# Cross attention on one core: the first pass in pairs of matmuls on two 64-row halves of a 128-row stack, each pair set right behind a group of value sums

## The reference, cut to what matters

```python
q = split_heads(x @ qw + qb)            # 2 batches, 16 heads, 256 queries, width 16
k = split_heads(ctx @ kw + kb)          # 4096 keys
v = split_heads(ctx @ vw + vb)
scores = einsum('bqhd,bkhd->bhqk', q, k) / 4 + mask      # layer 0
scores = einsum(...) * 16**-0.5 + (i - j) * w_rel[h]     # layer 1: a bias by distance
out = einsum('bhqk,bkhd->bqhd', softmax(scores), v)
```

## Time and profile before

| what | value |
|---|---|
| device time, median of 3 | 1697.72 us (1696.73 to 1702.26) |
| profiled execution, from first to last instruction | 1696.4 us |
| granted TensorE clock, mean | 0.979 |
| PE busy | 1610.3 us (95%) |
| DVE busy | 1139.9 us (67%) |
| ACT busy | 861.8 us (51%) |
| the two cross attentions (first exponential to last copy of sums) | 258 to 656 us and 1114 to 1513 us |

### The profile page before, as it was taken

One profiled execution on the slowest core, in us unless ns is written; L12 is line 12 of the kernel. 1 busy time (PEld: TensorE's weight loads), 2 busy tenths in 40 slices (PEclk: granted clock), 3 DMA queues, 4 the chain that ended last, 5 costly groups with the idle time before them and its releaser, 6 DMA issues. The chain is left out here.

```text
span 1696.4 us, 36130 instructions
## 1 busy us (share of the span) xinstructions
PE 1610.3 (95%) x12499; PEld 972.6 (57%) x12509; DVE 1139.9 (67%) x2013; ACT 861.8 (51%) x1784; POOL 287.9 (17%) x372
## 2 busy tenths in 40 slices
PE   9999999999999997998989999889999999989697
PEld 4444444544545444674868999644454454545496
DVE  6777788888888884738553111388888888845621
ACT  3222216777777775742531111257777777765332
POOL 1422220000000001020202444220000000000053
PEclk9999999999999999999989999989999999999898
DMA  6578756434334324300038999753443434204075
GB/s 204 179 204 219 207 164 135 67 56 71 59 62 68 56 38 135 60 1 1 1 132 267 335 309 311 231 94 58 70 61 59 71 56 66 46 1 102 13 219 143
DMA packets 150745, 196.29 MB, mean 116 GB/s; under 512 B 30426, under 2 KB 123964, under 8 KB 144624
## 3 DMA queue, kind: packets, MB, share of 16 engines
q1 hardware_dynamic: 141864, 188.83, 45.3%
q0 software_dynamic: 6720, 4.31, 1.5%
q10 hardware_dynamic: 2064, 1.87, 0.3%
HBM read 156.49 MB, written 41.39 MB: 117 GB/s over the span
## 5 line engine op out<-in xcount | busy, mean ns | idle before, releaser
L1225 ACT ACTIVATE probs<-ps 128x512 f32<-128x512 f32 x1024 | 558.4, 599 | 179.0 <-PE ps L1128 166.6
L1251 DVE TENSOR_REDUCE top<-ps 128x1 f32<-128x1024 f32 x504 | 594.1, 1220 | 61.4 <-PE ps L1107 47.6
L1128 PE MATMUL ps<-qst,kst 105*128 105x256 bf16 x2048 | 353.9, 276 | 7.6 <-DVE qst L1256 2.5
L1107 PE MATMUL ps<-kst,qst 105*128 105x512 bf16 x1008 | 305.0, 385 | 6.6 <-DVE top L1251 4.0
L1128 PEld LDWEIGHTS ps<-qst,kst 105*128 105x128 bf16 x2048 | 170.3, 100 | 228.0 <-ACT probs L1225 87.1
L1142 PE MATMUL ps_o<-probs,vst 128*32 128x256 f32 x4096 | 274.1, 385 | 2.3 <-ACT probs L1225 2.3
L1142 PEld LDWEIGHTS ps_o<-probs,vst 128*32 128x32 f32 x4096 | 106.8, 109 | 113.2 <-issue 50.9
L383 POOL COPY vst<-vall 128x512 f32 (+1 forms) x64 | 39.4, 615 | 697.5 <-PE ps_o L1142 694.4
L2350 PE MATMUL ps_h<-xe,vall 128*128 128x80 f32 x1024 | 149.6, 265 | 0.0
L2350 PEld LDWEIGHTS ps_h<-xe,vall 128*128 128x128 f32 x1024 | 136.4, 191 | 0.1
L1107 PEld LDWEIGHTS ps<-kst,qst 105*128 105x128 bf16 x1008 | 88.5, 98 | 63.5 <-issue 29.5
(11 more groups left out here) (444 smaller groups left out, 2011.4 us busy)
## 6 DMA issues: line engine op xcount, KB each, us to landing
kst<-kd SPq DMA_DIRECT2D x372, 128.0 KB
kd<-probs SPq DMA_DIRECT2D x64, 384.0 KB, 2.9
vall<-in_L_ffn_wg_dram SPq DMA_DIRECT2D x32, 512.0 KB, 6.0
vall<-in_L_ffn_wu_dram SPq DMA_DIRECT2D x32, 512.0 KB, 7.9
vall<-in_L_ffn_wd_dram SPq DMA_DIRECT2D x32, 512.0 KB, 6.1
w<-in_L_ffn_w_dram SPq DMA_DIRECT2D x16, 1024.0 KB, 7.6
vd<-square_weights SPq DMA_DIRECT2D x16, 512.0 KB, 4.1
vall<-vd SPq DMA_DIRECT2D x16, 512.0 KB, 6.2
```

Of the source, the lines that this page charges most:

```text
L1107: mm = pe.matmul(ps1[:, slot1(m, u), x * 512:(x + 1) * 512], qst[:, m, qt * P:(qt + 1) * P], kst[:, m, c * W1 + x * 512:c * W1 + (x + 1) * ...
L1128: mm = pe.matmul(ps2[:, SCORES2[u], x, :], kst[:, m, kt * P:(kt + 1) * P], qst[:, m, :], start=True, stop=True)
L1225: nc.scalar.activation(probs[:, u % SLOTS, :, :], ps2[:, SCORES2[u], :, :], ACT.Exp).then_inc(probs_ready, 1)
L1251: v.tensor_reduce(top[:, b, qt, c:c + 1], ps1[:, slot1(m, u), :], AX, ALU.max).then_inc(mx, 1)
```

## The change

Keys and queries are laid out anew on all 128 rows. Rows 0 to 63 and rows 64 to 127 each hold a set of pieces that gives the score of the first pass alone; all 128 together still give the score of the second pass. The second half of the queries for the first pass lies in a stack of its own, `q1st`, which one more DMA per head fills (`second_q`); the rest of its rows is zero.

A first-pass unit is now one matmul of 512 keys on rows 0 to 63 and one of the other 512 keys on rows 64 to 127, into two banks. Two units stand together, right behind each of the four groups of value sums. The groups stand behind units 1, 6, 10 and 14, so that the second pass goes in runs of 5, 4, 4 and 3 units (the last run includes unit 0 of the next head). The finish and the turning of the maximum both stand behind unit 14, after the sums and the pairs. Their targets in PSUM move from `ps1` to slot 0 of `ps2`.

Off PE: POOL splits the maximum into pieces, in four small operations (`c_rows`). ACT copies the turned maximum into the stack and the turned sums to memory (`raw`), both before the exponential of unit 15. DVE keeps the maxima and one joining operation per head, and divides once for four heads. Keys are loaded with nine DMAs instead of six, and queries with eight instead of six per half; zero rows are loaded once per layer.

```diff
@@ -283,8 +282,12 @@
 
 
 NBUF = 4
-K_PIECES = (0, 0, 0, 1, 1, 2)
-Q_PIECES = (0, 1, 2, 0, 1, 0)
+
+KEY_ROWS = ((3, 2, 0, 7), (10, 0, 0, DH), (26, 0, 0, DH), (42, 1, 0, DH),
+            (64, 2, 14, DH), (67, 2, 7, 14), (74, 0, 0, DH), (90, 0, 0, DH), (106, 1, 0, DH))
+Q_ROWS = ((3, 0, 0, 7), (10, 0, 0, DH), (26, 1, 0, DH), (42, 0, 0, DH),
+          (64, 0, 14, DH), (67, 0, 7, 14), (74, 2, 0, DH), (106, 1, 0, DH))
+ZERO_ROWS = ((CROW, NPIECE), (ZROW, 1), (90, DH), (AUXROW + HALF, 6))
 HC = H // C
 SLOTS = 8
...
 
     def load_k(self, eng, L, h, m, first=0, last=SK, signal=None):
-        for r, piece in enumerate(K_PIECES):
-            eng.dma_start(self.kst[r * DH:(r + 1) * DH, m, first:last],
-                          self.pr.kd[L][piece, ds(h * DH, DH), (m % B) * SK + first:(m % B) * SK + last]).then_inc(
+        for r, piece, d0, d1 in KEY_ROWS:
+            eng.dma_start(self.kst[r:r + d1 - d0, m, first:last],
+                          self.pr.kd[L][piece, ds(h * DH + d0, d1 - d0),
...
+    def second_q(self, eng, h, m, b):
+        eng.dma_start(self.q1st[HALF + Q1ROW:P, m, :], self.qall[Q1ROW:HALF, ds(h, 1), b, :].rearrange(
+            "r o q -> r (o q)")).then_inc(self.q1_in[m], 16)
+
...
+        zero = self.pr.inp["qaux"][0:1, :]
+        for r, n in ZERO_ROWS:
+            eng.dma_start(self.qall[r:r + n, :, :, :].rearrange("r h b q -> r (h b) q"),
+                          bc(zero.broadcast_to([n, S]), 1, H * B)).then_inc(self.aux_in, 16)
         for b in range(B):
-            aux = bc(self.pr.inp["qaux"], 1, H) if self.L == 0 else self.pr.qaux_dram.rearrange("h r q -> r h q")
-            eng.dma_start(self.qall[CROW:XROWS, :, b, :], aux).then_inc(self.aux_in, 16)
+            aux = (bc(self.pr.inp["qaux"][3:9, :], 1, H) if self.L == 0 else
+                   self.pr.qaux_dram[:, 3:9, :].rearrange("h r q -> r h q"))
...
+                        if c == 0:
+                            sp.wait_ge(buffers.q1_cleared, 1)
+                            sp.wait_ge(buffers.aux_in, buffers.n_q_aux)
+                            sp.wait_ge(buffers.q_in[0], 16 * len(Q_ROWS))
+                            for m in range(FIRST, NBUF):
+                                buffers.second_q(sp, m // B, m, m % B)
...
                 with sp.Fori(1, NG // NBUF) as h2:
                     for m in range(NBUF):
-                        g, h, _, _ = head_number(h2, m)
+                        g, h, _, b = head_number(h2, m)
                         wait_at(pr, sp, sc2, N2 * (g - NBUF + 1))
+                        buffers.second_q(sp, h, m, b)
                         buffers.keys.load_k(sp, buffers.L, h, m)
...
+                def c_rows(n):
+
+                    pool.wait_ge(c_max, n)
+                    link = Chain(pool, c_steps, C_STEPS * n - C_STEPS)
+                    g = nc.gpsimd
+                    whole, rest, nought = buffers.cwhole[:, :], buffers.crest[:, :], buffers.nought[:, :]
+                    link(g.tensor_tensor(cp[:, :, 0], whole, nought, ALU.add))
+                    link(g.tensor_tensor(rest, whole, cp[:, :, 0], ALU.subtract))
+                    link(g.tensor_tensor(cp[:, :, 1], rest, nought, ALU.add))
+                    link(g.tensor_tensor(cp[:, :, 2], rest, cp[:, :, 1], ALU.subtract))
+
                 def copy_first_v(m):
                     if made_here:
...
-                def pass1(g, m, b, u, wait=True, finished=True):
+                def pass1(g, m, u, wait=True):
...
-                    if u == 6:
-                        pe.wait_ge(mx, N1 * g + u)
-                    elif u == 7 and finished:
-                        pe.wait_ge(o_done, 2 * (g - 1))
-                    elif wait:
+                            pe.wait_ge(buffers.q1_in[m], 4 * (g - m) + (16 if m >= (FIRST if made_here else 1) else 0))
+                    if wait:
                         pe.wait_ge(mx, N1 * g + u - 1)
...
+                    whole = made_here and isinstance(g, int) and g < FIRST
                     for x in range(W1 // 512):
-                        mm = pe.matmul(ps1[:, slot1(m, u), x * 512:(x + 1) * 512], qst[:, m, qt * P:(qt + 1) * P],
-                                       kst[:, m, c * W1 + x * 512:c * W1 + (x + 1) * 512], start=True, stop=True)
+                        rows = slice(0, P) if whole else slice(x * HALF, (x + 1) * HALF)
+                        queries = q1st if x and not whole else qst
+                        mm = pe.matmul(ps1[:, u % 2, x * 512:(x + 1) * 512], queries[rows, m, qt * P:(qt + 1) * P],
+                                       kst[rows, m, c * W1 + x * 512:c * W1 + (x + 1) * 512], start=True, stop=True)
                     mm.then_inc(sc1, 1)
...
-                    pe.wait_ge(c_chain, CHAIN * g + CHAIN)
-                    if not (isinstance(g, int) and g == 0):
+                    if isinstance(g, int) and g == 0:
+                        pe.wait_ge(c_first, CHAIN)
+                    else:
+                        pe.wait_ge(c_steps, C_STEPS * g)
                         pe.wait_ge(probs_ready, N2 * (g - 1) + C_AFTER + 1)
...
 
                     pe.wait_ge(o_copied, g + 1)
-                    if ahead:
-                        pe.wait_ge(mx, N1 * (g + 2) + 5)
-                    else:
-                        pe.wait_ge(mx, N1 * NG)
-                        pe.wait_ge(o_done, 2 * g)
+                    pe.wait_ge(probs_ready, N2 * g + N2 + (C_AFTER + 1 if not (isinstance(g, int) and g == NG - 1) else 0))
                     for qt in range(QT):
-                        mm = pe.matmul(ps_f[1 - b][:, qt, :], o_sb[:, b, qt * P:(qt + 1) * P], pr.cf("sel4"),
+                        mm = pe.matmul(ps_f[:, qt, :], o_sb[:, b, qt * P:(qt + 1) * P], pr.cf("sel4"),
                                        start=True, stop=True)
...
                     for u in range(N2):
                         pass2(g, m, b, u, wait=not (first and u < 3))
-                        if u in SUMS_AT and SUMS_AT.index(u) < NPV - 1:
+                        if u == LAST_SUMS_AT and not first:
+                            pv_group(g - 1, 1 - b, NPV - 1)
+                        if u == 0 and first:
+                            for i in range(2, 4):
+                                pass1(g + 1, (m + 1) % NBUF, i)
+                        if u in SUMS_AT:
                             pv_group(g, b, SUMS_AT.index(u), first)
-                        if u == FINISH_AT and not first:
-                            finish(g - 1, 1 - b, ahead=not last)
                         if u in PASS1_AT and not last:
-                            pass1(g + 1, (m + 1) % NBUF, 1 - b, 2 + PASS1_AT.index(u), finished=not first)
+                            for i in range(2):
+                                pass1(g + 1, (m + 1) % NBUF, 4 + 2 * PASS1_AT.index(u) + i)
                         if u in NEXT_AT and not last and place != "last but one":
-                            pass1(g + 2, (m + 2) % NBUF, b, NEXT_AT.index(u))
-                        if u == SUMS_AT[-1] and not first:
-                            pv_group(g - 1, 1 - b, NPV - 1)
+                            for i in range(2):
+                                pass1(g + 2, (m + 2) % NBUF, 2 * NEXT_AT.index(u) + i)
+                        if u == TURN_AT and not first:
+                            finish(g - 1, 1 - b)
                         if u == TURN_AT and not last:
                             turn_c(g + 1)
 
-
-
-                SUMS_AT, FINISH_AT, TURN_AT = (6, 11, 13, 0), 7, 14
-                PASS1_AT, NEXT_AT = (0, 1, 2, 5, 9, 10), (11, 15)
+                LAST_SUMS_AT, SUMS_AT, TURN_AT = 1, (6, 10, 14), 14
+                PASS1_AT, NEXT_AT = (1, 6), (10, 14)
...
+                def copy_c(g, m):
+                    act.wait_ge(c_turned, g + 1)
+                    nc.scalar.copy(qst[CROW:CROW + NPIECE, m, :], ps_c[0:NPIECE, :]).then_inc(c_ready, 1)
+
                 def head(g, h, m, b, place):
                     for u in range(N2):
-                        if u == 1 and place != "first":
+                        if u == 2 and place != "first":
                             copy_o(g - 1, 1 - b)
+                        if u == N2 - 1 and place != "first":
+                            act.wait_ge(o_turned, g)
+                            if place != "last":
+                                act.wait_ge(c_turned, g + 2)
+                            nc.scalar.copy(raw[:, :, 1 - b, ds((h - 1 if b == 0 else h) * (DH + 1), DH + 1)],
+                                           ps_f[:, :, 0:DH + 1]).then_inc(raw_ready, 1)
+                        if u == N2 - 1 and place != "last":
+                            copy_c(g + 1, (m + 1) % NBUF)
...
+                    v.tensor_reduce(top[:, b, qt, c:c + 1], ps1[:, u % 2, :], AX, ALU.max).then_inc(mx, 1)
+
+                def greatest(g, b):
+                    dve.wait_ge(mx, N1 * g + N1)
```

(81 more changed lines are left out.)

142 lines of the change are left out of this document (73 added, 69 removed).

## The result

The changed kernel takes 1747.24 us, median of 4 runs (1746.22 to 1748.25), beside 1697.93 us of the kernel before: 1.0294 times as long, 95% interval 1.0281 to 1.0306. The profiled execution's span is 1746.4 us, before 1696.4.

The account below looks back on a forecast made before the run. PE's strict order, with waits for slots, ACT and the copied maximum, was taken as the bound: 13.05 us a head, 0.51 more. 58 x 0.51 = 29.6 us on the 1696.4 span, plus 1.3, gave 1727 us, range 1678 to 1757.

Parts of the forecast that it names:

- poor overlap: First-pass pairs on PE: the two row halves overlap little or not at all; without overlap 1828 us; chance 0.13.
- something off PE comes late: POOL's steps, second queries or ACT's copies late: 0.4 us a head more, 1750 us; chance 0.07.
- What bounds a head: PE's strict order, with waits for three slots and ACT; 13.05 us a head, though PE's own work falls to 10.5.
- 2.94, 2.94, 3.42 and 3.75: Sums-to-sums stages on PE, in us: two runs of four, the run of five, the end of a head.
- Pairs overlap, 1.73: First-pass units on PE: row halves run side by side, 0.22 instead of 0.44 a unit, 1.73 us less a head.
- Eight switches of 0.10: Four visits to the pairs on PE: entering and leaving 64-row mode costs about 0.10 us each, bounds 0 and 0.10.
- rival of cheap switches: 64-row mode on PE entered and left for nothing: 12.25 us a head, 1681 us; chance 0.20.
- 58 x 0.51 = 29.6: Full heads of both layers, 29 intervals each: 0.51 us more a head, 29.6 us in all.
- I take 0 for both layer starts and keep +3 as bound.: Starts of both layers: extra DMA issues cost nothing, though layer 1's query cover shrinks from 5.4 us to 2 or 3.
- DMAs at 48%: Loads in the heads: ten issues instead of six raise DMA time from 41% to some 48%, with cover over a head.
- POOL's cover 3.7 us: Between the joined maximum and the turning: 3.7 us of cover for POOL's four steps, put at 0.8 to 1.8 us.
- Finish 0.39: Finish on PE at the end of a head: takes 0.39 us and pays no switch.

Follow-up runs that it names:

- halves in turn: The changed kernel with both 512-key halves of a first-pass unit on rows 0 to 63; 1855.42 us, 1.0902 of the kernel before.
- full_height: The changed kernel with every first-pass matmul on all 128 rows, in the same order; 1825.89 us, 1.0724 of the kernel before.
- after_again: The changed kernel itself measured once more, unedited, as yardstick on another chip; 1750.41 us, 1.0290 of the kernel before.
- pool_twice: The changed kernel with POOL's four small steps done twice over; 1752.77 us, 1.0303 of the kernel before.
- both_start: The changed kernel with constant key rows loaded over blocks 5 to 8 and layer 0's zero rows written by one POOL memset; 1744.43 us.
- turn_ahead: both_start with the pairs inside the runs, and finish and turning moved ahead of the sums behind unit 14; 1630.64 us, 0.9577 of the kernel before.

## Why the prediction was right, and where it fell short

- *The number.* The forecast of 1727 us came out low: the loss is 49.3 us by the medians, where 29.6 were summed up. 1747.2 lies 5 above the own range of this case, 1712 to 1742. It lies within 1678 to 1757 because that range was widened for rivals that didn't happen (poor overlap, something late in each head), and that part is luck. The 1750 of "something off PE comes late" is near by chance: nothing of it happened in the heads.
- *What bounds a head.* Right: a strict chain on PE through slots, not PE's busy time. The stages came within 0.01 us of 2.94, 2.94, 3.42 and 3.75; moving the pairs took 1.71 us out of a head, in which PE's work grew. (Of first-pass units, three and not four stand between two groups of sums in the order shown of the kernel before.)
- *Pairs overlap, 1.73.* Right: 1.72 by the halves in turn.
- *Eight switches of 0.10.* Right: 0.09 for the exit by the rows of full_height and of the changed kernel, 0.43 instead of 0.22 for a pair visited alone. The rival of cheap switches falls. The Trainium skill's "TensorEngine Tiling (Array Packing)", section Key Properties, by which a change of mode drains the engine, agrees for row halves too; the page was followed in the sum.
- *Heads, 58 x 0.51 = 29.6.* Measured 32.9. A head is 13.07, not 13.05 (1.2 us). The heads that stand outside the loop were shorter before than the 12.54 taken for all: the first three intervals of layer 0 took (308.2 - 271.1) / 3 = 12.4, and after they take as long as the others within 0.1. The last two heads, taken as unchanged, cost 0.2 a layer.
- *"I take 0 for both layer starts and keep +3 as bound."* This is the term that failed: 15.1 and 4.2 us, 19.3 together, two fifths of the loss, of which 13.1 are lost in the projection of layer 0. The mistake was to look for the DMAs' cost in the heads, and at layer 1's start in the cover of the queries. What each issue is queued ahead of on SP in the projection, the key stores, wasn't asked. The runs show the zero rows and the doubled key rows there; the repair brought the first copy from 283.1 to 273.6. A second part was put at nothing too: the first head of a layer stands ahead of the first copy, outside the 29 intervals, and takes 2.0 us more in layer 0 from the start of its first pass to its copy.
- *DMAs at 48%.* Not needed and not reached: 43% in the heads.
- *POOL's cover 3.7 us.* Right: in the profile the steps start at 475.52 and the turning at 479.37, 3.85. The steps take 1.04 of it, so 2.8 are left when they end, at 476.55.
- *Finish 0.39.* It takes 0.49 behind the 64-row mode. It didn't show in the sum of the end of a head, 3.76, since other terms were high by as much, and that is luck: ACT starts its second copy 0.09 behind the first (479.79, 479.88), where I took 0.18, and PE goes on 0.48 behind that start, where I took 0.37 + 0.14.

Left open: the 4.2 us before layer 1. The trace shows PE waiting 1.55 us at 1155.79 for the second queries, which are loaded from rows that were themselves just loaded. No run took this load away. In after_again the stretch takes 2.5 more than before with a wait of 1.44 in it, in pool_twice 1.1 more and in both_start 3.5 more, both without such a wait. So it differs by 3 us between profiles of one order, and the wait doesn't explain it alone. What made the loads behind the zero rows slow isn't shown either, only that it went with them.

## What to carry to other kernels

In a strict order on one engine, filler work belongs where the engine would otherwise wait, not where it saves a mode switch: here the pairs inside the runs cost four switches more, 0.4 us a head, and took away 2.1 of waits. When a change adds transfers, list for each queue what stands behind them at the place of issue, set-up phases included; a few loads of many short rows can hold back stores that have nothing to do with them. And after each gain look for the next cover that is used up, as POOL's chain in turn_ahead.

## What the runs showed of the hardware beyond expectation

- Two bf16 matmuls on rows 0 to 63 and 64 to 127 start within a hundredth of a microsecond of each other, and 512 columns of the pair take 0.22 us, as one full-height matmul does.
- A float32 finish of four matmuls takes 0.39 us where its first weight load runs 0.11 ahead of it, and 0.49 to 0.50 where the load starts with it: behind a change of mode, and in turn_ahead also without one.
- Four loads of rows of zeros, each fed from one short row, took 3.46 us to issue and made the next ones slow: 4.54 us for two, 4.83 for the first two of the small key rows, which take some 0.3 each otherwise. With the zero rows written by POOL instead, the same two groups took 2.48 and 0.68.
